# Reordering the openings, the seams and the tail of a feed-forward, convolution, attention and feed-forward kernel

## The chip, the cores and the metric

The kernel runs on one core of one Trainium2 chip. The metric is the device time of one execution in microseconds. All matrix products are done by TensorE (PE); VectorE (DVE), ScalarE (ACT) and GpSimd (POOL) do elementwise work, and SyncE (SP) issues the DMAs. Work on different engines is ordered by semaphores that the program sets and waits for by hand.

## The reference

A block of three layers over 2048 tokens of 1024 features in float32, each added to its input. The first and third are the same feed-forward, the second is a convolution with block attention:

```python
def _L0_ffn_ref(x, weight, bias, gate_w, in_channel_scale, out_channel_scale):
    xf = x.reshape(-1, H)
    router_logits = xf @ gate_w.T
    routing = jax.nn.softmax(router_logits.astype(jnp.float32), axis=1).astype(x.dtype)
    in_scale = routing @ in_channel_scale
    out_scale = routing @ out_channel_scale
    wb = ste_sign(weight)
    out = xf * in_scale @ wb.T * out_scale + bias
    return out.reshape(B, S, -1)

x = x + 0.5 * _L0_ffn_ref(_layernorm(x, axis=-1), ...)
x = x + _L0_attn_ref(_layernorm(x, axis=-1), ...)   # convolution of 3 taps to q, k, v of 256 channels; 16 heads in blocks of 128
x = x + 0.5 * _L0_ffn_ref(_layernorm(x, axis=-1), ...)
```

## The kernel before, in words

**Feed-forward** (`feed_forward`, used twice). The tokens go in 8 blocks of 256 (`NG`), each of two tiles of 128. For a block: the tile is normalised by VectorE (`stats`, GpSimd's `power` for the inverse root, `normalise`), transposed by TensorE in four pieces (`transposes`, one bank of PSUM for blocks from 2 on, so each piece waits until ScalarE's `copy_t` has emptied the one before), multiplied with the gate (`logits`, folded by `logits_back`), turned into a routing by VectorE's `softmax_begin` and `softmax_end`, and transposed back (`routing`). Then, for each of 8 slices of 128 features, TensorE makes the input scale (`in_scale`), VectorE multiplies it in (`scale`), ScalarE rounds it to a high part (`high`) and VectorE takes the low part (`low`). The product with the signed weights has four quarters `q` for a block: two tiles by two halves of 512 outputs. A quarter is `product(g, p, q, 0, 8)`: for each of 8 `k` one matmul with the high and one with the low part, 16 matmuls of 512 columns. Quarters use two banks in turn; a quarter waits until the one two before has been scaled out of its bank by VectorE (`m_scaled`), and `in_scale` waits for a low part made earlier (`lo_done`), since it reuses its bank. GpSimd adds half the bias to the residual (line 299) and the residual to the scaled product (line 309). SyncE stores a block of 1 MB when its four quarters are done.

These steps are software-pipelined by hand: while block g's quarters are multiplied, block g+1 is scaled, g+2 gets its logits and routing, g+3 is normalised and transposed. Each engine's `body(g, p)` writes down its order for one block. The first block is an exception, an opening: block 2's transposes and block 1's routing stand in the middle of quarter 0's product, behind k 5.

**End of the first feed-forward.** Its output is normalised again and goes into `X` for the convolution. The last block goes tile by tile (`last_stats`, `last_normalise`, `difference`), while TensorE already does the part of the convolution that needs only earlier blocks (`early_product`); `first_filter` and GpSimd's `outer_sum` make its filters from a raw load, and `early_data` and `late_data` its data.

**Convolution** (`conv_phase`). It is done in 3 stages of 6 units (`NCH`), unit n having two halves h of 4 chunks, for two results f. Filter i = 4n + 2h + f lies in a ring of 3. In stage 0 the products are single float32 products. In stages 1 and 2 each is made of three products of high and low parts: ScalarE makes the high and VectorE (`finish`, line 1232) the low part of the filter, and VectorE makes the low parts of 16 pieces of data (`second_low`, `third_low`) at each seam. `sums(n)` makes two filters of stage 1 from loaded ones. A load into one of two rooms is issued when `sums` of the pair before last is done. `add(n)` combines the finished unit n into `Y`; for stage 1 these are six operations, of which two work in PSUM and four add into `Y`.

**Attention**, behind it, is not touched.

## Time and profile before

| | us |
|---|---|
| median of 3 runs | 978.25 (975.35 to 980.58) |
| the profiled execution | 976.29 |
| its span, first to last instruction | 974.5 |
| mean granted TensorE clock | 0.986 |

| engine | busy us | share |
|---|---|---|
| TensorE matmul | 907.2 | 93% |
| VectorE | 694.1 | 71% |
| GpSimd | 454.3 | 47% |
| ScalarE | 418.8 | 43% |

The trace is of one execution. Its times count from the first instruction. "Idle before" is the time in which an engine did nothing ahead of an instruction, with the work that released it. The first feed-forward lasts until about 215 us, the convolution until 447, the attention until 805, the second feed-forward to the end.

### The profile page before, as it was taken

Reading aid. Unit: us, or ns where it says so; the run is one execution under the profiler, and the core shown is the slowest. Engines: PE = TensorE matmul, PEld = TensorE weight load, DVE = VectorE, ACT = ScalarE, POOL = GpSimd, SP = SyncE. Lnnn points to the kernel's source line nnn. Section 1 sums busy time; section 2 is a strip of 40 time slices with the busy share of each in tenths; the row PEclk is TensorE's granted clock in tenths of the full one; section 3 lists DMA queues with packets and bytes.
Section 4 is the critical chain, followed back from the end, with each engine's and each line's share of the span. In section 5 each row is a group of like instructions: output and inputs, shape, how many; then the busy total and the mean of one; then the engine's idle time right before and its main releaser. Section 6 shows DMA issues by size and latency. Waiting matters only on the chain.

```text
span 974.5 us, 15517 instructions
## 1 busy us (share of the span) xinstructions
PE 907.2 (93%) x4992; PEld 695.5 (71%) x4992; DVE 694.1 (71%) x1449; ACT 418.8 (43%) x1127; POOL 454.3 (47%) x587
## 2 busy tenths in 40 slices
PE   4799999998999999999989999999999798999997
PEld 3477777775444787887777787887777676877785
DVE  5788887688998888455683686288289786776651
ACT  3534443421234336234773565367256443333331
POOL 1267777787763330000255255247144543555565
PEclk9899999998999999999999999999999998999999
DMA  9433322433234431864012124023244652444333
GB/s 283 182 130 130 130 87 88 144 127 109 98 103 156 162 119 44 313 227 173 1 44 65 44 56 141 1 77 96 94 91 139 212 198 86 145 134 149 130 108 108
DMA packets 43013, 119.98 MB, mean 123 GB/s; under 512 B 7232, under 2 KB 16448, under 8 KB 41536
## 3 DMA queue, kind: packets, MB, share of 16 engines
q1 hardware_dynamic: 42944, 119.11, 37.1%
q8 instruction: 37, 0.61, 0.2%
q14 instruction: 32, 0.26, 0.1%
HBM read 87.64 MB, written 31.46 MB: 122 GB/s over the span
## 4 chain that ended last, share of the span: by engine, by line
PE 70%; DVE 16%; issue 5%; ACT 4%; POOL 4%; DMA 1%; DVEq 0%; POOLq 0%; ACTq 0%
PE a_p_g L1925 19%; PE a_p_g L681 12%; PE f_p_m L681 9%; PE a_p_s L1949 4%; PE c_p_m L1353 3%; PE c_p_m L1355 3%; PE c_p_m L1354 3%; PE c_p_m L1351 3%; PE a_p_o L1973 3%; PE a_p_t L1959 2%; PE f_p_t L622 2%; DVE a_oT_lo L1852 1%; PE a_p_s L622 1%; ACT f_xT L549 1%; ACT a_s L1727 1%
## 5 line engine op out<-in xcount | busy, mean ns | idle before, releaser
L1653 POOL TENSOR_TENSOR a_s<-a_s,a_sums 128x512 f32<-128x512 f32 x64 | 66.6, 1041 | 232.9 <-DVE a_sums L1832 232.9
L309 POOL TENSOR_TENSOR f_y<-f_y,f_res 128x256 f32<-128x256 f32 x128 | 96.9, 778 | 114.8 <-DVE f_y L536 114.0
L1727 ACT ACTIVATE a_s<-a_s,a_nmx 128x128 f32<-128x128 f32 x256 | 99.5, 391 | 48.6 <-DVE a_nmx L1828 48.5
L681 PE MATMUL f_p_m<-f_wsign,f_a_hi 128*128 128x512 f32 x256 | 105.8, 413 | 0.0
L681 PE MATMUL a_p_g<-f_wsign,f_a_hi 128*128 128x512 f32 x256 | 103.2, 403 | 0.0
L681 PE MATMUL f_p_m<-f_wsign,f_a_lo 128*128 128x512 f32 x256 | 101.9, 398 | 0.0
L681 PE MATMUL a_p_g<-f_wsign,f_a_lo 128*128 128x512 f32 x256 | 101.1, 395 | 0.0
L299 POOL TENSOR_TENSOR f_res<-f_res,f_hbias 128x256 f32<-128x256 f32 x128 | 96.0, 771 | 0.0
L1925 PE MATMUL a_p_g<-c_xs_hi,x_room 128*128 128x512 f32 x256 | 94.7, 416 | 0.0
L1353 PE MATMUL c_p_m<-c_vh,c_ring 128*128 128x512 f32 x192 | 75.5, 393 | 5.3 <-issue 3.0
L1351 PE MATMUL c_p_m<-c_vf,c_ring_f 128*128 128x512 f32 (+1 forms) x192 | 73.8, 542 | 1.3 <-DVE c_ring_f L1019 1.1
L1355 PE MATMUL c_p_m<-c_vh,c_ring 128*128 128x512 f32 x192 | 74.8, 389 | 0.0
L1354 PE MATMUL c_p_m<-c_vl,c_ring 128*128 128x512 f32 x192 | 74.8, 389 | 0.0
L1011 POOL TENSOR_TENSOR c_raw<-c_raw 128x256 f32<-128x256 f32 x48 | 46.3, 984 | 53.9 <-DMA c_raw<-in_conv_w_dram 42.1
L1351 PEld LDWEIGHTS c_p_m<-c_vf,c_ring_f 128*128 128x128 f32 x192 | 33.5, 190 | 41.3 <-issue 36.8
L1639 POOL TENSOR_TENSOR a_residual<-a_residual,a_bps 128x256 f32<-128x256 f32 x56 | 41.3, 774 | 42.3 <-DMA a_residual<-x_after_ffn 42.3
L1823 DVE TENSOR_TENSOR a_s<-a_p_s,a_mask 128x512 f32<-128x512 f32 x64 | 43.8, 685 | 20.0 <-PE a_p_s L1949 19.7
L1925 PEld LDWEIGHTS a_p_g<-c_xs_hi,x_room 128*128 128x128 f32 x256 | 48.4, 189 | 13.5 <-issue 0.7
L681 PEld LDWEIGHTS f_p_m<-f_wsign,f_a_hi 128*128 128x128 f32 x256 | 48.9, 191 | 11.9 <-issue 2.1
L681 PEld LDWEIGHTS a_p_g<-f_wsign,f_a_hi 128*128 128x128 f32 x256 | 48.7, 190 | 11.9 <-issue 2.1
L681 PEld LDWEIGHTS a_p_g<-f_wsign,f_a_lo 128*128 128x128 f32 x256 | 48.7, 190 | 8.7
L681 PEld LDWEIGHTS f_p_m<-f_wsign,f_a_lo 128*128 128x128 f32 x256 | 49.0, 192 | 7.9
(223 smaller groups left out, 2204.7 us busy)
## 6 DMA issues: line engine op xcount, KB each, us to landing
c_raw<-in_conv_w_dram SPq DMA_DIRECT2D x24, 768.0 KB, 4.3
f_w_raw<-in_w_t_dram SPq DMA_DIRECT2D x8, 1024.0 KB, 9.3
f_res<-in_x_dram SPq DMA_DIRECT2D x16, 512.0 KB, 3.9
x_after_ffn<-f_y SPq DMA_DIRECT2D x8, 1024.0 KB, 6.1
f_xin<-x_after_attention SPq DMA_DIRECT2D x8, 1024.0 KB, 5.0
f_res<-x_after_attention SPq DMA_DIRECT2D x16, 512.0 KB, 4.1
out_dram<-f_y SPq DMA_DIRECT2D x8, 1024.0 KB, 6.3
f_xin<-in_x_dram SPq DMA_DIRECT2D x7, 1024.0 KB, 5.2
```

The costliest lines, as they stand in the source:

```text
L299: last = pool.tensor_tensor(res[:, t, part], res[:, t, part], hbias[:, part], ALU.add)
L309: last = pool.tensor_tensor(y[:, p, t, part], y[:, p, t, part], res[:, t, part], ALU.add)
L681: last = pe.matmul(p_m[:, q % 2, :], part[p][:, k, q // 2 * P:q // 2 * P + P], wsign[:, k, q % 2 * HALF:q % 2 * HALF + HALF], start=(k == ...
L1011: last = pool.tensor_tensor(self.raw[:, h, 0, part], self.raw[:, h, 0, part], self.raw[:, h, 2, part], ALU.add)
L1351: last = pe.matmul(out[:, quads], conv.half(i)[:, cols], vf[:, f, k, quads], start=start, stop=stop)
L1353: pe.matmul(out, ring[:, slot, 0, cols], vh[:, f, k, :], start=start, stop=False)
L1354: pe.matmul(out, ring[:, slot, 0, cols], vl[:, f, k, :], start=False, stop=False)
L1355: last = pe.matmul(out, ring[:, slot, 1, cols], vh[:, f, k, :], start=False, stop=stop)
L1653: pool.tensor_tensor(s[:, r], s[:, r], sums[:, r].unsqueeze(2).broadcast_to([P, 4, P]), ALU.mult).then_inc(probs_ready, 1)
L1727: done = act.activation(s[:, r, h, :], s[:, r, h, :], ACT.Exp, bias=nmx[:, r, h:h + 1], scale=SCALE, accum_out=sums[:, r, h:h + 1])
L1823: dve.tensor_tensor(s[:, r], p_s[:, u % 2, :].rearrange("p (h t) -> p h t", h=4), mask[:].unsqueeze(1).broadcast_to([P, 4, P]), ALU.add).t ...
L1925: mm = pe.matmul(p_g[:, bank, :], a, b, start=n == 0, stop=n == len(pairs) - 1)
```

## The change

In words, in the order of the diff:

- The last quarter's residual of each feed-forward is added by VectorE (`last_sum`), not by GpSimd. In the first, GpSimd's second filter sum moves behind its bias sum.
- The last block of the second feed-forward is stored in three pieces (`store_last`): tile 0, and the two halves of tile 1. The first keeps its store.
- The opening of both (`opening`): quarter 1's product no longer stands behind block 2's transposes. Its k 0 to 3 are taken in turns with quarter 0's k 4 to 7 ahead of the first transpose, and its other k stand between the transposes, the input scales and the logits. `copy_t(2, ...)` moves into ScalarE's body with its copies and high parts between, and `copy_logits(2)` moves from q = 0 to q = 1. Two k of quarter 2 come ahead of its input scale.
- In the first feed-forward, `normalise(2, 0)` stands ahead of `softmax_end(1)`.
- In the convolution, `add` of stage 1 is split into `combine` (two operations) and `accumulate` (four), and the low part `finish(n, 1)` stands between. At both seams low parts of filters come ahead of part of the low parts of the data.

The core of the diff:

```diff
+        def store_last():
+            g, p = NG - 1, (NG - 1) % 2
+            sp.wait_ge(y_done, 4 * g + 2)
+            sp.dma_start(dstv[g][:, 0, :], y[:, p, 0, :]).then_inc(y_stored[p], 16)
+            for q, h in enumerate((slice(0, HALF), slice(HALF, D))):
+                sp.wait_ge(y_done, 4 * g + 3 + q)
+                sp.dma_start(dstv[g][:, 1, h], y[:, p, 1, h]).then_inc(y_stored[p], 16)
...
-                pool.wait_ge(res_biased, 4 * g + q + 1)
-                pool.wait_ge(m_scaled, 4 * g + q + 1)
-                for part in halves(h):
-                    last = pool.tensor_tensor(y[:, p, t, part], y[:, p, t, part], res[:, t, part], ALU.add)
-                last.then_inc(y_done, 1)
+                if q < 3 or not late(g):
+                    pool.wait_ge(res_biased, 4 * g + q + 1)
+                    pool.wait_ge(m_scaled, 4 * g + q + 1)
+                    for part in halves(h):
+                        last = pool.tensor_tensor(y[:, p, t, part], y[:, p, t, part], res[:, t, part], ALU.add)
+                    last.then_inc(y_done, 1)
+                if q == 3 and X is not None and late(g):
+                    conv.outer_sum(pool, 1)
...
-                if q == 2 and X is not None and late(g):
-                    conv.outer_sum(pool, 1)
...
+        def last_sum():
+            g, p = NG - 1, (NG - 1) % 2
+            dve.wait_ge(res_biased, 4 * NG)
+            dve.wait_ge(m_scaled, 4 * NG)
+            dve.wait_ge(y_done, 4 * NG - 1)
+            dve.tensor_tensor(y[:, p, FT - 1, HALF:D], y[:, p, FT - 1, HALF:D], res[:, FT - 1, HALF:D], ALU.add).then_inc(y_done, 1)
...
                 if first_round(g) and q == 0:
+                    copy_t(2, 0, 0)
+                    copy_t(2, 0, 1)
                     copy_routing(1, 1)
+                    copy_t(2, 0, 2)
+                    high(1, 1, 0)
+                    copy_t(2, 0, 3)
+                    high(1, 1, 1)
+                    continue
...
-                if q == 0 and exists(g + 2):
+                if q == (1 if first_round(g) else 0) and exists(g + 2):
                     copy_logits(g + 2)
...
+        def opening(g, p):
+            out_scale(g, p, 0)
+            product(g, p, 0, 0, 4)
+            for k in range(4, KD):
+                product(g, p, 1, k - 4, k - 3)
+                product(g, p, 0, k, k + 1)
+            transposes(2, 0, 0)
+            product(g, p, 1, 4, 5)
+            transposes(2, 0, 1)
+            product(g, p, 1, 5, 6)
+            routing(1)
+            transposes(2, 0, 2)
+            in_scale(1, 1, 0)
+            transposes(2, 0, 3)
+            product(g, p, 1, 6, 7)
+            in_scale(1, 1, 1)
+            out_scale(g, p, 1)
+            logits(2, 0)
+            product(g, p, 1, 7, KD)
+            in_scale(1, 1, 2)
+            logits_back(2)
+            in_scale(1, 1, 3)
+            transposes(3, 1, 0)
...
-            for q in range(4):
+            if first_round(g):
+                opening(g, p)
+            for q in range(2 if first_round(g) else 0, 4):
                 out_scale(g, p, q)
...
+                ahead = 2 if first_round(g) and q == 2 else 0
+                product(g, p, q, 0, ahead)
...
             f.stats(2, 0)
+            f.normalise(2, 0)
             f.softmax_end(1)
-            f.normalise(2, 0)
             f.stats(3, 1)
             group_loop(dve, f.body)
             f.last_normalise(0)
             conv.early_data(dve, Xp, 1)
+            f.last_sum()
             f.last_stats(1)
...
             sums(2 * NCH)
-            for r in range(8):
+            for r in range(6):
                 second_low(r)
             finish(2 * NCH, 0)
+            for r in range(6, 8):
+                second_low(r)
+            finish(2 * NCH, 1)
             sums(2 * NCH + 1)
             for r in range(8, 12):
                 second_low(r)
-            finish(2 * NCH, 1)
-            second_low(12)
             finish(2 * NCH + 1, 0)
-            for r in range(13, 16):
+            for r in range(12, 16):
                 second_low(r)
+            finish(2 * NCH + 1, 1)
             add(NCH - 1)
-            finish(2 * NCH + 1, 1)
             sums(2 * NCH + 2)
             for n in range(2 * NCH + 2, 4 * NCH):
                 if n + 1 < 4 * NCH:
                     sums(n + 1)
                 finish(n, 0)
                 if n % 2:
-                    add((n - 3) // 2)
+                    combine((n - 3) // 2)
                 finish(n, 1)
-            for r in range(8):
+                if n % 2:
+                    accumulate((n - 3) // 2)
+            for r in range(6):
                 third_low(r)
             for n in range(4 * NCH, PAIRS):
                 finish(n, 0)
                 if n == 4 * NCH:
-                    for r in range(8, 12):
+                    for r in range(6, 12):
                         third_low(r)
-                if n % 2:
+                if n == 4 * NCH + 1:
+                    combine((n - 3) // 2)
+                elif n % 2:
                     add((n - 3) // 2)
                 finish(n, 1)
+                if n == 4 * NCH + 1:
+                    accumulate((n - 3) // 2)
```

## Rows read from the trace of the kernel before

**Rows 1.** The page, part 1: busy us (share of the span), instructions.

```profile
PE 907.2 (93%) x4992; PEld 695.5 (71%) x4992; DVE 694.1 (71%) x1449; ACT 418.8 (43%) x1127; POOL 454.3 (47%) x587
```

**Rows 2.** Waits of TensorE: us in total, times, longest us.

```profile
PE f_p_t L622 <- DVE f_xin L365: 13.9, 2, 11.0
...
PE f_p_n L700 <- DVE f_res L471: 3.0, 1, 3.0
```

**Rows 3.** Timeline of TensorE, first opening: start us, us, instruction, idle before.

```profile
36.96 1.12 PE L622 MATMUL f_p_t<-ident,f_xin 128*128 128x128 f32 x4 [2.93 <-DVE f_xin L365]
...
54.43 0.36 PE L662 MATMUL c_p_m<-f_rT,f_ics 128*128 128x256 f32 x1 [0.74 <-DVE f_a_lo L423]
```

**Rows 4.** Timeline of VectorE, same stretch.

```profile
35.14 1.76 DVE L365 TENSOR_SCALAR f_xin<-f_xin,f_mv,f_rstd 128x1024 f32<-128x1024 f32 x2
36.94 2.47 DVE L344 BATCH_NORM_STATS2 f_st<-f_xin 128x6 f32<-128x512 f32 x4
...
46.30 0.42 DVE L423 TENSOR_TENSOR f_a_lo<-c_p_m,f_a_hi 128x256 fp32r<-128x256 f32 x1 [1.28 <-ACT f_a_hi L566]
...
53.87 0.41 DVE L423 TENSOR_TENSOR f_a_lo<-c_p_m,f_a_hi 128x256 fp32r<-128x256 f32 x1
```

**Rows 5.** Timeline of GpSimd, same stretch.

```profile
34.02 0.69 POOL L279 TENSOR_TENSOR f_rstd<-f_vpe,f_minus_half 128x2 f32<-128x2 f32 x1 [19.18 <-DVE f_vpe L356]
```

**Rows 6.** Stretches: start:end, us, TensorE busy (matmuls), granted clock, DMA, GB/s.

```profile
29.95:33.36 3.41, 3.41 (x10) 0.51 0.77 309
33.36:36.78 3.42, 0.67 (x3) 0.99 0.01 6
...
40.19:43.60 3.41, 1.88 (x12) 0.99 0.00 0
...
811.60:815.01 3.41, 1.42 (x13) 1.00 0.22 26
```

**Rows 7.** Timeline of ScalarE, second opening.

```profile
810.39 0.58 ACT L549 COPY f_xT<-a_p_s 128x512 f32<-128x512 f32 x1 [0.81 <-PE a_p_s L622]
```

**Rows 8.** The chain that ended last, second opening: start us, us, work.

```profile
819.05 3.21 PE a_p_g L681 x8
...
822.39 1.82 PE a_p_g L681 x8
```

**Rows 9.** Timeline of VectorE, second opening.

```profile
817.45 0.42 DVE L423 TENSOR_TENSOR f_a_lo<-a_p_o,f_a_hi 128x256 fp32r<-128x256 f32 x1 [2.02 <-ACT f_a_hi L566]
```

**Rows 10.** Timeline of all engines, end of the first feed-forward.

```profile
217.63 2.83 POOL L299 TENSOR_TENSOR f_res<-f_res,f_hbias 128x256 f32<-128x256 f32 x2
...
221.98 1.28 DVE L459 BATCH_NORM_STATS2 f_nst<-f_y 128x6 f32<-128x512 f32 x2 [2.09 <-POOL f_y L309]
```

**Rows 11.** One line's instructions: ns min/median/max, first and last start, shapes.

```profile
L1206 DVE SCALAR_TENSOR_TENSOR X<-X,c_room x8: 681/1212/1219, 240.5 to 292.3; 128x512 f32<-128x512 f32 x8
```

**Rows 12.** Timeline of TensorE, stage 0 of the convolution.

```profile
274.14 14.34 PE L1351 MATMUL c_p_m<-c_vf,c_ring_f 128*128 128x512 f32 x32 [0.37 <-DVE c_ring_f L1019]
```

**Rows 13.** The chain that ended last, first seam of the convolution.

```profile
320.81 4.26 DMA c_raw<-in_conv_w_dram
```

**Rows 14.** Timeline of TensorE, units 7 and 12 of the convolution.

```profile
332.74 0.50 PE L1353 MATMUL c_p_m<-c_vh,c_ring 128*128 128x512 f32 x1 [1.16 <-DVE c_ring L1232]
...
380.11 0.47 PE L1353 MATMUL c_p_m<-c_vh,c_ring 128*128 128x512 f32 x1 [0.79 <-issue]
...
390.28 0.50 PE L1353 MATMUL c_p_m<-c_vh,c_ring 128*128 128x512 f32 x1 [1.17 <-DVE c_ring L1232]
```

**Rows 15.** Timeline of all engines, the end.

```profile
968.61 1.40 POOL L309 TENSOR_TENSOR f_y<-f_y,f_res 128x256 f32<-128x256 f32 x2 [1.03 <-DVE f_y L536]
970.03 0.40 SPq L226 DMA_DIRECT2D out_dram<-f_y  x1
```

**Rows 16.** DMA issues: number, KB each, median us to landing.

```profile
x_after_attention<-a_residual SPq DMA_DIRECT2D x56, 128.0 KB, 2.3
```

**Rows 17.** Stretches of the end: us, engines' busy us, granted clock, DMA share, GB/s.

```profile
973.00:973.50 0.50, 0.00 (x0) 0.00 (x0) 0.00 (x0) 0.00 (x0) 0.00 (x0) 0.50 1.00 401
```

More of the change, by code:

```diff
@@ L244, in stored @@
         def stored():
-            for count in y_stored:
-                sp.wait_ge(count, 16 * (NG // 2) + 1)
-        return SyncSteps(load_x, load_tiles, load_gate, load_scales, load_w, load_bias, load_res, store, stored, body)
+            for p, count in enumerate(y_stored):
+                pieces = 2 if X is None and p == (NG - 1) % 2 else 0
+                sp.wait_ge(count, 16 * (NG // 2 + pieces) + 1)
+        return SyncSteps(load_x, load_tiles, load_gate, load_scales, load_w, load_bias, load_res, store, store_last, stored, body)
     def pool(pool):
@@ L539, in vector @@
         return VectorSteps(start, constants, tile_stats, mean_var, stats, normalise_tile, normalise, scale_parts,
-                           softmax_begin, softmax_end, softmax, scale, low, None if X is None else last_stats, None if X is None else last_normalise,
+                           softmax_begin, softmax_end, softmax, scale, low, last_sum, None if X is None else last_stats, None if X is None else last_normalise,
                            None if X is None else difference, body)
@@ L701, in normed @@
             last.then_inc(n_full, 1)
+        def opening(g, p):
[21 more added lines that the diff above has]
+            transposes(3, 1, 0)
         def body(g, p):
-            for q in range(4):
+            if first_round(g):
+                opening(g, p)
+            for q in range(2 if first_round(g) else 0, 4):
                 out_scale(g, p, q)
-                first = first_round(g) and q == 0
-                if first:
-                    product(g, p, q, 0, KD - 2)
-                    for piece in range(4):
-                        transposes(2, 0, piece)
-                        if piece < 2:
-                            product(g, p, q, KD - 2 + piece, KD - 1 + piece)
-                    routing(1)
+                ahead = 2 if first_round(g) and q == 2 else 0
+                product(g, p, q, 0, ahead)
                 if exists(g + 1):
@@ L728, in body @@
                 else:
-                    if not first:
-                        product(g, p, q, 0, 4)
+                    product(g, p, q, ahead, 4)
                     if exists(g + 1):
@@ L736, in body @@
                         logits_back(g + 2)
-                    if not first:
-                        product(g, p, q, 4, KD)
+                    product(g, p, q, 4, KD)
                 if q and exists(g + 3):
@@ L857, in _ @@
                 f.sign_w(k)
-            for q in range(4):
-                f.copy_t(2, 0, q)
             group_loop(act, f.body)
@@ L1776, in _ @@
             s2.exponent(1)
-            for piece in range(4):
-                s2.copy_t(2, 0, piece)
             group_loop(act, s2.body)
```

33 lines of the change are left out of this document (19 added, 14 removed).

## The prediction

> **What bounds the kernel now.** The page comes first. TensorE is busy for 907.2 of 974.5 us, VectorE for 71% (the page; [rows 1]). So an edit can only win where TensorE stands still or runs at the low clock. The list of who waited for whom gives where: 2.9 us for a normalised tile in the first opening, 3.0 us for the last tile's normalised residual, and a handful of waits of about 1 us on the convolution's filters [rows 2, 14]. Second, the timelines of TensorE and VectorE at each of these places tell what came last, and third, the stretches with a low granted clock tell what the standstill costs afterwards. Elsewhere the products run back to back at 0.227 us each (8 in 1.82 us [rows 8]), and none falls away. The five places are separate, and behind each TensorE hardly waits, so I add their shifts.
>
> **1. Opening of the first feed-forward (-4.0 us).** Before, quarter 0's product is cut by the transposes of block 2; after, 12 matmuls of quarter 1 are put ahead of the first transpose, and quarter 1's other k go between transposes, scales and logits. TensorE before: it stops at 33.97, waits 2.93 us for the normalised tile, and gets the fifth input scale of block 1 (the one that waits for a low part) at 54.43 [rows 3]. What ends last on that way is VectorE: low part 0 at 46.30, from there a queue without a wait over 0.5 us to low part 3 at 53.87, whose end releases 54.43 [rows 4]. This queue keeps its order, so TensorE at 54.43 moves by as much as the 46.30 moves.
>
> When does it start now? The variance is ready at 33.87, GpSimd's power ends at 34.71 [rows 5]. `normalise(2, 0)` now stands ahead of `softmax_end`, so it runs from 34.8 to 36.5 (1.76 us [rows 4]) instead of 36.9. The eight small operations of `softmax_end` took 1.4 us from 33.78 and 2.1 us from 50.55, when GpSimd was at work; it halves the bias in the new place, so they end at 37.9 to 38.6. Statistics of block 3 take 3.0 us [rows 4]: 40.9 to 41.6. TensorE in the meantime: 24 matmuls from 29.47. The clock is low from 29.95 to 33.36 [rows 6], in which 8 go at 0.43 us; the other 14 take 3.2 us, so the first transpose stands at 36.55, just as the tile is ready. The extra matmuls cost nothing there: they lie in the 2.93 us hole. Then the transposes are paced by ScalarE's copy, 1.39 us apart as in the second opening (0.58 and 0.81 idle [rows 7]): 36.6, 38.0, 39.4 and, after the copy of the routing, 40.6; input scale 0 is out at 39.9, before VectorE is free for it. So VectorE scales at 41.2 (middle), and low part 0 follows 0.86 us later (as 49.35 to 50.21) at 42.1, against 46.30: 4.2 us. In the before it took 1.71 us there, because ScalarE stood behind the logits; `copy_logits(2)` now comes one quarter later. I take off 0.2 us for block 3's normalising beside GpSimd's bias sum: 4.0, between 3.2 and 4.6.
>
> What is late next: TensorE has quarter 2's k 0 to 3 to do, from the release of the bank (VectorE's sum of quarter 0, 48.75 before, 44.7 now) to 47.1, and then stands until 50.4 for low part 3. That is the standstill of before, put in one piece of about 3 us.
>
> **2. Opening of the second (-2.7 us).** No wait for a tile there: the first transpose came at 808.36 and now comes at 805.63 + 24 x 0.227 = 811.1, so 2.7 us later. Before, four transposes 1.4 us apart, the copies of scales and routing and the slow logits brought low part 0 to 817.45 and low part 3 to 825.38, and TensorE, delayed by quarter 1 at the low clock, reached the scale only at 826.66, 0.86 us after it could [rows 7 to 9]. Now: transposes at 811.1 and 812.5, routing at 813.3, its copy until 814.05, scale 0 on TensorE at 814.2, VectorE at 814.5, low part 0 at 815.4: 2.0 us earlier, low part 3 ends at 823.8, TensorE goes on at 823.9 instead of 826.66, if nothing else is late. 2.7, between 1.8 and 3.2.
>
> **3. The granted clock (+1.7 us).** Stretches in which TensorE was busy for 0.67 and 1.42 us of 3.4 us were followed by one or two of that length at 0.51 of full speed; one with 1.88 us was not [rows 6]. Each low stretch of 3.4 us loses 1.7 us of products (8 take 3.21 instead of 1.82 us [rows 8]). Both new standstills (3.3 and 3.1 us) can fall either side of that; I count one drop of 3.4 us in the two openings, and none or two for the range (0 to +3.4). The low stretch at 815 to 822 belongs to the before and is already inside term 2.
>
> **4. End of the first feed-forward (-0.9 us).** Before, the chain is: VectorE's product of the last quarter, GpSimd's filter sum (215.81, 1.85 us), bias sum (2.83 us), residual sum (1.40 us) until 221.94, statistics, power, normalising until 225.18, TensorE at 225.24 [rows 2, 10]. Now GpSimd's bias sum goes ahead of the filter sum, and VectorE adds the residual itself behind `early_data(1)`, which ends at 219.88. The sum of 128x512 takes 0.68 us, or 1.21 where GpSimd works beside it [rows 11]; so the statistics start at 220.5 to 221.1 against 221.98. Queued behind the new wait on VectorE are the statistics, two differences, two filters and the data; its semaphore has been given by about 217.7 if the bias sum takes the 1.85 us that the filter sum took in that place. The filter sum moves to 217.7 to 220.5, and its first reader is at 225.10: hidden. I take 0.9, range 0 to 1.4.
> The Trainium skill speaks against this part (SBUF — State Buffer, Who interferes with whom): a VectorE operation with two SBUF inputs and a GpSimd operation that reads SBUF block each other for the whole instruction. The trace agrees with the two lengths of 0.68 and 1.21 us, and with 5.33 us for the filter sums at 228.87; by the rule alone the gain would be 0.3 less than by the middle of the rows.
> Behind it the first stage of the convolution is VectorE's: its period is 14.70 us without a wait, TensorE waits 0.37 us in each [rows 12]. So TensorE gains what VectorE gains there, though its own low clock at 224.5 to 231.3 may go: that is no gain.
>
> **5. The convolution's seams (-1.0 us).** From stage 0 to 1, the filters' low parts put ahead of data let unit 6 start at 309.8 instead of 310.67, and its second half without the 1.25 us wait: 2.1 us. But from 302.93 to 320.7 VectorE has no wait over 0.1 us, and the order of its work is all that changes: `sums(14)` still ends at 320.8. This releases a filter load (4.26 us), GpSimd's sum, and `sums(16)` at 326.61, and behind it the filter half that TensorE needs at 328.60 [rows 13]. So the 2.1 us are waited for there. The split of `add` gives the next half 2.4 us earlier and takes away the wait of 1.16 us at 332.74 [rows 14], but VectorE is again full until 335.3, where unit 8's filter is due at 335.5: 0.1 us is left. Together 0.1.
> From stage 1 to 2: before, `finish(23,1)` at 373.91 stands behind the sums; ScalarE has its high part at 371.84, so VectorE loses 0.35 us. Unit 12's first low part then comes two data parts earlier, at 378.5 instead of 379.33: TensorE starts unit 12 0.85 us earlier (0.79 us wait [rows 14]). Its second filter comes after all 12 data parts as before, 0.35 us later, which takes that back. Then `combine` and the low part of filter 25 go ahead of the four sums: ready at 388.2, TensorE needs it at 389.2, instead of 390.28 with 1.17 us wait. Behind that stage 2 is TensorE's. So 1.1 there, less what the first seam may cost: 1.0, between 0.2 and 2.5.
>
> **6. The end (-2.4 us).** Before: product until 968.46 on VectorE, GpSimd 968.61 to 970.01, store of 1 MB issued 970.03, data moving until 973.53 at about 400 GB/s, end at 974.5 [rows 15, 17]. Now VectorE adds in 0.69 us and ends at 969.2 (-0.8). The last store holds 256 KB: 2.6 us of data become 0.65 (-1.95) if the half rows of 2 KB go as fast. The bound on the other side is the 2.3 us median of 128 KB stores against 4.0 here [rows 15, 16], a slope of 2.0 us per MB, so -1.5. The other 768 KB are issued at 962.4 and 966.2 and done before. Sum 2.3 to 2.75; I take 2.4, range 1.9 to 2.9.
> The Trainium skill (DMA: Bandwidth & Descriptors, Bandwidth) has a rule against pieces: batch DMAs to 1 MiB or more. It would count if the queue were full; the trace shows none of it in use from 967 to 970. No term changes.
>
> **Sum.** -4.0 - 2.7 + 1.7 - 0.9 - 1.0 - 2.4 = -9.3 us. The profiled execution took 976.29 us (span 974.5, 1.8 around it): 967.0. It lies 1.96 us below the median of 978.25 (975.35 to 980.58), from which it would be 968.95. Where the clock falls differs between executions, so I take the middle: 968.0. About 0.5% (4.9 us) is what a measurement of this kernel can tell from no change.
>
> **The rivals.**
> A, the forecast: gains of 7.5 to 11.5 us, 0.50.
> B, the openings stay at full clock, or the first conv seam keeps its 2.1 us since the load at 320.81 comes earlier than I count: -11.0 to -14, about 965.5. For it: TensorE is busy in the new seams with products, not only transposes. Against: the holes of 3 us. 0.14.
> C, ScalarE or the clock takes part of the openings back: the copy of the fourth transposed piece now stands behind `high(1, 1, 0)`, which waits for VectorE's scale. The logits, their copy and their fold are ready at about 45.4, VectorE wants them at 45.6 in the first opening; each microsecond more there is one lost. With two low stretches besides: 9.3 - 1.7 - 2 = 5.6, so 972. 0.20.
> D, the change doesn't do what it says: the holes are only moved. If low part 0 of both openings comes no earlier, since transposes that stand behind 24 matmuls are 2.7 us later, terms 1 and 2 are 0 to -1 and the clock costs 0 to +1.7: -3.5 to -4.5, 974.2. For it: VectorE bounds both. Against: four waits on the way to low part 0 are removed in the first. 0.13.
> E, slower than before: the standstill in one piece lets the clock fall in the rounds behind both openings and it stays low there. Against: in each of its places before, it came back after at most two stretches [rows 6]. Each microsecond at low clock costs half of one, so it decides from the point at which more than 22 us of low clock are added; over both first rounds (some 20 us each) the price is 20 + the 1.7 not counted twice: -11 + 20, so 986. 0.03.
> Range: 962.0 to 974.0 leaves out E, half of D and the end of B. Faster by more than 0.5%: A, B and most of C, 0.85; within: 0.12; slower: 0.03.
>
> **What would show it.** Term 1: first transpose of block 2 at about 36.6 behind 24 matmuls, VectorE's low part 0 near 42, TensorE idle up to 3.3 us before a scale, and quarter 3's start 4 us earlier. Term 2: the same at 10 us behind the opening's start. Term 3: a stretch at 0.5 of the clock right behind the idle one. Term 4: statistics right behind VectorE's own sum, POOL's filter sum beside the data. Term 5: no wait at unit 6, but 1.5 us at unit 7's start and 0.4 in it. Term 6: three stores, the last 2.3 us from issue to landing. The prediction is wrong if VectorE's queue in the openings is not the order-giver, or if the load behind `sums(14)` comes earlier.

## The result, and the profile after

| | before | after |
|---|---|---|
| median of four runs each, same chip | 977.53 us | 966.09 us (963.99 to 969.31) |
| profiled execution | 976.29 | 963.99 |
| its span | 974.5 | 962.2 |

The ratio is 0.9884, 95% interval 0.9843 to 0.9924: 11.3 us less, between 7.4 and 15.3. In a second series (six runs of after, eleven of before) it was 0.9892 (0.9869 to 0.9916). The forecast of 968.0 stands inside both intervals, near the end of the smaller gain.

In what follows, "before" and "after" are the kernels without and with the change, and "the hole" is the wait of TensorE for low part 3 of block 1 in each new opening.

The page of after. Columns: busy us (share of the span) and instructions; [rows 1] has those of before. TensorE is busy for 8 us less in a span 12.3 us shorter.

```profile
PE 899.2 (93%) x4992; PEld 690.5 (72%) x4992; DVE 695.2 (72%) x1451; ACT 418.3 (43%) x1127; POOL 451.6 (47%) x583
```

The list of TensorE's waits in after (us in total, times, longest). Against [rows 2], the 2.93 us for a tile in the first opening and the 3.0 us for the last tile are no longer in it, and two waits of 2.4 us for a low part (line 433) are new, one in each opening.

```profile
...
PE c_p_m L686 <- DVE f_a_lo L433: 2.7, 2, 2.4
PE c_p_m L1409 <- DVE c_ring L1273: 2.5, 3, 1.3
...
PE a_p_o L686 <- DVE f_a_lo L433: 2.4, 1, 2.4
```

**First opening.** TensorE's timeline in after: the last product ahead of the fifth input scale, that scale, two of the products behind it, quarter 3's output scale. It answers to [rows 3], where the scale stood at 54.43.

```profile
45.82 0.39 PE L705 MATMUL f_p_m<-f_wsign,f_a_lo 128*128 128x512 f32 x1
48.57 0.55 PE L686 MATMUL c_p_m<-f_rT,f_ics 128*128 128x256 f32 x1 [2.36 <-DVE f_a_lo L433]
48.92 0.63 PE L705 MATMUL f_p_m<-f_wsign,f_a_hi 128*128 128x512 f32 x1
49.35 0.63 PE L705 MATMUL f_p_m<-f_wsign,f_a_lo 128*128 128x512 f32 x1
...
52.36 0.48 PE L693 MATMUL c_p_m<-f_ocs,f_rT 128*128 128x512 f32 x1
```

And VectorE's, with low part 0 (46.30 before, [rows 4]), the six rows of `softmax_end` (lines 405 to 417) and low part 3, which releases the scale:

```profile
39.86 0.42 DVE L433 TENSOR_TENSOR f_a_lo<-c_p_m,f_a_hi 128x256 fp32r<-128x256 f32 x1 [0.44 <-ACT f_a_hi L583]
...
44.36 0.42 DVE L433 TENSOR_TENSOR f_a_lo<-c_p_m,f_a_hi 128x256 fp32r<-128x256 f32 x1 [0.15 <-ACT f_a_hi L583]
44.70 0.16 DVE L405 TENSOR_REDUCE f_r_sum<-f_r_exp 128x2 f32<-128x16 f32 x1
44.89 0.17 DVE L407 RECIPROCAL f_r_max<-f_r_sum 128x2 f32<-128x2 f32 x1
45.09 0.17 DVE L409 TENSOR_TENSOR f_r_exp<-f_r_exp,f_r_max 128x16 f32<-128x16 f32 x1
45.30 0.60 DVE L412 CAST f_r_hi<-f_r_exp 128x16 fp32r<-128x16 f32 x1
45.94 0.73 DVE L415 COPY f_rt<-f_r_hi 128x16 f32<-128x16 f32 x2
46.58 0.24 DVE L417 TENSOR_TENSOR f_rt<-f_r_exp,f_r_hi 128x16 f32<-128x16 f32 x2
...
48.01 0.41 DVE L433 TENSOR_TENSOR f_a_lo<-c_p_m,f_a_hi 128x256 fp32r<-128x256 f32 x1
```

The scale moved by 5.86 us, of which 1.57 us is the start-up, ahead of anything the change touches (VectorE's subtraction in `softmax_begin` at 30.80 before, 29.23 after): 4.29 us between the two kernels, at clocks that were not equal (see term 1 below). Behind the hole the products start 0.43 us apart, not 0.23. The stretches (start:end, us, TensorE busy, granted clock, DMA, GB/s) give the clock:

```profile
44.00:48.00 4.00, 2.13 (x9) 1.00 0.01 5
48.00:52.00 4.00, 3.43 (x9) 0.57 0.39 125
52.00:56.00 4.00, 4.00 (x25) 1.00 0.02 8
```

TensorE stood still, then it was granted half the clock (1.2 GHz) for 3.4 us, then 2.4 GHz again.

**Second opening.** The scale stands at 815.42 behind a like hole, and the clock falls at 816.2. The first row is that of before, where it stood at 826.66; [rows 8] shows the slow products ahead of it.

```profile
826.66 0.28 PE L662 MATMUL a_p_o<-f_rT,f_ics 128*128 128x256 f32 x1
...
815.42 0.36 PE L686 MATMUL a_p_o<-f_rT,f_ics 128*128 128x256 f32 x1 [2.35 <-DVE f_a_lo L433]
```

**End of the first feed-forward.** VectorE's own sum (line 468), the statistics right behind, GpSimd's bias and filter sums (lines 308, 1052), and TensorE's transposes, which stood at 225.24 before. [rows 2, 10] has the chain of before, except for its GpSimd residual sum, which is the first row here:

```profile
220.54 1.40 POOL L309 TENSOR_TENSOR f_y<-f_y,f_res 128x256 f32<-128x256 f32 x2
...
211.33 1.86 POOL L308 TENSOR_TENSOR f_res<-f_res,f_hbias 128x256 f32<-128x256 f32 x2
213.15 2.84 POOL L1052 TENSOR_TENSOR c_raw<-c_raw 128x256 f32<-128x256 f32 x2
...
215.33 1.21 DVE L468 TENSOR_TENSOR f_y<-f_y,f_res 128x512 f32<-128x512 f32 x1
216.57 1.28 DVE L476 BATCH_NORM_STATS2 f_nst<-f_y 128x6 f32<-128x512 f32 x2
...
219.83 0.66 PE L724 MATMUL f_p_n<-ident,f_res 128*128 128x128 f32 x4 [2.11 <-DVE f_res L488]
```

**First conv seam.** GpSimd's filter sum behind the load that `sums(14)` releases, `sums(16)`, and TensorE's waits at unit 7, in it, and at unit 8. The last two rows are unit 12 of after, in the second seam (380.11 before, [rows 14]), and unit 8 of before.

```profile
319.61 1.43 POOL L1052 TENSOR_TENSOR c_raw<-c_raw 128x256 f32<-128x256 f32 x2 [6.20 <-DMA c_raw<-in_conv_w_dram]
...
321.07 0.70 DVE L1262 TENSOR_TENSOR c_p_u<-c_raw 128x512 f32<-128x512 f32 x1 [3.56 <-POOL c_raw L1052]
...
317.07 0.47 PE L1409 MATMUL c_p_m<-c_vh,c_ring 128*128 128x512 f32 x1 [1.26 <-DVE c_ring L1273]
323.02 0.50 PE L1409 MATMUL c_p_m<-c_vh,c_ring 128*128 128x512 f32 x1 [0.25 <-DVE c_ring L1273]
329.78 0.47 PE L1409 MATMUL c_p_m<-c_vh,c_ring 128*128 128x512 f32 x1 [1.02 <-DVE c_ring L1273]
...
377.74 0.47 PE L1409 MATMUL c_p_m<-c_vh,c_ring 128*128 128x512 f32 x1 [1.23 <-issue]
...
335.64 0.39 PE L1353 MATMUL c_p_m<-c_vh,c_ring 128*128 128x512 f32 x1
```

**The end.** VectorE's last product, its sum, the issue of the last store, and the data of it (columns as above, all engines idle, clock, DMA share, GB/s). [rows 15 to 17] have these of before.

```profile
958.21 0.69 DVE L553 TENSOR_TENSOR f_y<-a_p_g,f_oscale 128x512 f32<-128x512 f32 x1 [3.16 <-PE a_p_g L705]
959.00 0.69 DVE L468 TENSOR_TENSOR f_y<-f_y,f_res 128x512 f32<-128x512 f32 x1
959.71 0.33 SPq L234 DMA_DIRECT2D out_dram<-f_y  x1
...
960.50:961.00 0.50, 0.00 (x0) 0.00 (x0) 0.00 (x0) 0.00 (x0) 0.00 (x0) 1.00 0.89 348
```

**Where 12.3 us of span went**, by differences between the starts of the same instructions in both traces:

| stretch | before | after | gain |
|---|---|---|---|
| to the first product of the first feed-forward (not in the change) | 29.47 | 28.07 | 1.40 |
| opening 1: from there to VectorE's scaling of quarter 3 | 32.44 | 29.38 | 3.06 |
| rest of its quarters | 153.08 | 153.07 | 0.01 |
| end of it, to the first sum into `Y` | 29.61 | 28.67 | 0.94 |
| from there to `combine` of stage 1's fifth unit | 125.72 | 125.39 | 0.33 |
| from there to the last sum into `Y` | 78.03 | 76.94 | 1.09 |
| attention (not in the change) | 356.97 | 354.93 | 2.04 |
| opening 2: from its first output scale to quarter 3's scaling | 28.77 | 28.05 | 0.72 |
| rest of its quarters | 133.68 | 133.71 | -0.03 |
| last product on VectorE to the end | 6.73 | 3.99 | 2.74 |

8.9 us lie in stretches that the change touches, together with what the clock did there; 3.4 us lie in the two stretches that it doesn't touch.

### The profile page after: what moved, and what is told of

Read it like the earlier page. It is cut to its first block, busy times and chain, and to the rows that moved or that the text cites. A ratio compares the mean times of both kernels' runs of the same rounds, so it can differ in the third digit from the quotient of the medians.

```text
span 962.2 us, 15524 instructions
## 1 busy us (share of the span) xinstructions
PE 899.2 (93%) x4992; PEld 690.5 (72%) x4992; DVE 695.2 (72%) x1451; ACT 418.3 (43%) x1127; POOL 451.6 (47%) x583
## 4 chain that ended last, share of the span: by engine, by line
PE 74%; DVE 13%; issue 5%; ACT 4%; POOL 2%; DMA 1%; DVEq 0%; ACTq 0%; POOLq 0%
PE a_p_g L1980 19%; PE a_p_g L705 12%; PE f_p_m L705 10%; PE c_p_m L1407 4%; PE c_p_m L1409 4%; PE c_p_m L1411 4%; PE c_p_m L1410 4%; PE a_p_s L2004 3%; PE a_p_o L2028 3%; PE a_p_t L2014 2%; DVE a_oT_lo L1906 1%; PE f_p_t L646 1%; PE a_p_s L646 1%; ACT f_xT L566 1%; ACT a_s L1783 1%
## 5 line engine op out<-in xcount | busy, mean ns | idle before, releaser
L319 POOL TENSOR_TENSOR f_y<-f_y,f_res 128x256 f32<-128x256 f32 x124 | 94.0, 779 | 109.5 <-DVE f_y L553 108.8
```

The costliest lines, as they stand in the source:

```text
L319: last = pool.tensor_tensor(y[:, p, t, part], y[:, p, t, part], res[:, t, part], ALU.add)
```

## The experiments

Eleven kernels ran, before and after among them. Where the order of work and the clock are the same, the stretches of the table agree between executions within 0.1 us, and the first seam within 0.2, so one profile each decides much that a median of runs, which scatters by 2 to 5 us, doesn't. The table gives for each profile five stretches of the table above, with the number of low-clock stretches (each 3.4 us at half the clock, so up to 1.7 us lost; one at the very start of opening 1 is counted too) in brackets, and for the first seam the time from the end of stage 0's last product on TensorE to `combine` of unit 6.

| profile | opening 1 | end of FF 1 | first seam | second seam, stage 2 | opening 2 | end | median us |
|---|---|---|---|---|---|---|---|
| before | 32.44 (2) | 29.61 | 18.70 | 78.03 | 28.77 (2) | 6.73 | see text |
| openings only | 30.61 (3) | 29.64 | 18.86 | 78.03 | 26.47 (0) | 6.74 | 972.75 |
| conv only | 34.15 (3) | 29.61 | 18.31 | 76.93 | 27.02 (0) | 6.75 | 976.68 |
| ends only | 34.23 (4) | 28.68 | 18.88 | 78.02 | 28.78 (2) | 4.02 | 974.97 |
| after | 29.38 (2) | 28.67 | 18.39 | 76.94 | 28.05 (1) | 3.99 | 966.09 |
| after, again | 29.75 (2) | 28.68 | 18.21 | 76.92 | 28.04 (1) | 3.94 | 966.54 |
| filler | 28.18 (1) | 28.69 | 19.84 | 76.90 | 26.44 (0) | 3.98 | 966.60 |
| filler, again | 28.15 (1) | 28.68 | 19.32 | 76.96 | 26.48 (0) | 3.99 | 964.38 |
| softmax later | 27.08 (0) | 28.68 | 18.33 | 76.91 | 25.37 (0) | 3.98 | 963.46 |
| sums(14) first | 29.74 (2) | 28.68 | 17.19 | 76.95 | 28.05 (1) | 4.02 | 964.67 |
| three undone | 29.89 (1) | 28.13 | 18.29 | 76.92 | 28.02 (1) | 5.94 | (970.22) |
| three mended | 27.04 (1) | 28.14 | 17.15 | 76.90 | 25.34 (0) | 4.00 | 960.67 |
| routing behind | 26.82 (1) | 28.14 | 17.10 | 76.90 | 25.37 (0) | 3.96 | 959.23 |

The kernel before had a median of 978.68 beside the first three and the first filler, 975.75 beside "after, again" to "sums(14) first", 977.57 beside the last three. "Three undone" was run once, so its 970.22 is no median.

**1. The openings alone.** The kernel before with the diff's changes to `opening`, TensorE's and ScalarE's `body`, the copies, and this on VectorE:

```diff
-            f.softmax_end(1)
             f.normalise(2, 0)
+            f.softmax_end(1)
```

> The kernel before with the two openings alone: quarter 1 in the seam, block 2's normalising ahead of softmax_end, the copies and logits in their new order. The convolution, both ends and the stores are as before. My account: in the first opening the fifth input scale is released at about 48.6 instead of 54.4 (5.8 us, of which some 1.5 us is where the start-up fell), in the second 2.4 us are won against the start of that phase, and each opening has a hole of about 2.4 us ahead of that scale, behind which 3.4 us run at the low clock (1.4 to 1.7 us lost in each). Together -3.6 us when both drops come, -6.7 when none does; in the median of several executions about 973. The rival, that the holes were only moved: low part 0 of block 1 in the first opening no more than 1 us earlier than 46.3, and a time within 1.5 us of the kernel before.

972.75 us, ratio 0.9944 (0.9929 to 0.9958): 5.5 us less. The scale stood at 48.95 behind 2.35 us, and at 821.15 in the second, behind 2.35 us, but there the clock stayed high. That the holes were only moved is refuted: low part 0 stood at 10.64 us behind VectorE's subtraction, in before at 15.50. And a hole alone doesn't decide about the clock.

**2. The convolution alone.** The diff's part in `conv_phase`.

> The kernel before with the reordered convolution seams alone. My account: -0.1 to -0.5 us in the seam from stage 0 to 1 (the start of unit 8, counted from the end of stage 0) and -1.1 us in the seam from 1 to 2, together -1.2 to -1.6 us, so about 976. TensorE doesn't wait at unit 6, but 1.2 to 1.5 us at unit 7. The rival, that the first seam keeps its 2.1 us: unit 8 starts 2 us earlier, about 974.5, and there is no wait of over 0.5 us at unit 7.

976.68 us, ratio 0.9972 (0.9953 to 0.9991), too coarse to tell the two apart. The stretches do: -1.1 in the second seam (76.93), and in the first 18.31, where profiles in the old order have 18.70, 18.86 and 18.88: about -0.5, with 0.2 us of scatter. TensorE waited 1.28, 0.24 and 1.07 us at unit 7, in it and at unit 8. The rival of 2.1 us falls.
This trace also corrects my second term. Its second opening is in the old order, and it is the only one of the kernels with that order where the clock stayed high. TensorE's timeline there:

```profile
824.56 0.35 PE L662 MATMUL a_p_o<-f_rT,f_ics 128*128 128x256 f32 x1 [0.76 <-DVE f_a_lo L423]
```

The opening's first output scale stood at 805.05, so the scale came 19.51 us behind it. In before that was 21.34 (826.66 - 805.32), in the changed orders with the hole 18.96 to 18.99. At an equal clock the reordering wins 0.54 us there, not 2.4.

**3. The two ends alone.** `last_sum`, the order of GpSimd's sums, and the store in pieces.

> The kernel before with the two ends alone: VectorE adds the residual of the last quarter, GpSimd's second filter sum stands behind its bias sum, the last block is stored in three pieces. My account: -0.9 us at the last tile of the first feed-forward (VectorE's sum takes 0.7 us alone and 1.2 us beside GpSimd) and -2.4 to -2.8 us from VectorE's last product to the end, so about 974.5. The rival, that VectorE's sum and GpSimd stand in each other's way: the last tile's transposes no earlier than before, and 0.9 us less gain.

974.97 us, ratio 0.9964 (0.9950 to 0.9979): 3.5 us less; 0.93 in the end of the first feed-forward and 2.71 in the end. As expected; the two effects were told apart only in experiment 7.

**4. Products in the hole.** After, with nine matmuls of 512 columns into `p_n`, which nothing reads then, ahead of the scale that waits:

```diff
                     product(g, p, q, ahead, 4)
+                    if ahead:
+                        filler(g, p, q, 9)
```

> The changed kernel with nine products more in each opening, just ahead of the input scale for which TensorE waits 2.4 us. They go to a bank that nothing reads, so no result changes; 9 x 0.227 = 2.04 us, less than the hole. If the low clock behind the hole is the answer to TensorE's standstill, the stretch behind it stays at full clock: products at 0.227 instead of 0.43 us, quarter 3 starts 1.4 us earlier in the first opening and 1.7 us in the second, and the kernel comes out some 3 us below the changed one (about 963). The scale itself comes no earlier. The rival, that the clock falls there for another reason (the transposes and 128-column work ahead, or all that was done in the opening): the stretch is low just the same, and the time stays at 966 or is up to 0.5 us longer.

> The kernel with nine products more in each opening once more, since its first profile showed both openings at full clock and yet no shorter time (966.6), with low stretches at 497 to 505 and 764 to 768 instead. If filling the hole is worth what it saves in the openings, the median is 1.5 to 3 us below the changed kernel's of this same call; if the drops come back elsewhere, within 0.7 us of it. Both openings are at full clock from the extra products on, either way.

TensorE's timeline of the first run: the nine products, the scale, and the next transposes, which stand behind the half quarter.

```profile
47.98 2.21 PE L729 MATMUL f_p_n<-f_wsign,f_a_hi 128*128 128x512 f32 x9
50.52 0.36 PE L686 MATMUL c_p_m<-f_rT,f_ics 128*128 128x256 f32 x1 [0.32 <-DVE f_a_lo L433]
...
52.55 0.60 PE L646 MATMUL f_p_t<-ident,f_xin 128*128 128x128 f32 x4
```

From the scale to those transposes 2.03 us, in after 3.44. In both profiles both openings stayed at 2.4 GHz behind the filler, 1.2 to 1.6 us shorter in the first and 1.6 in the second, with the scale no earlier. The openings without a hole in experiments 5, 8 and 9 had no drop there either, six of six. So the standstill is what the clock answers to here, and the two drops cost about 3 us. The medians don't confirm that: 966.60 (ratio 0.9876, interval 0.9849 to 0.9903) beside 966.09 in another series, and 964.38 (0.9885, 0.9860 to 0.9910) beside 966.54 in the same one. Part of it is seen: both filler profiles are 0.9 to 1.6 us longer in the first conv seam, where the load for its first filters came later (VectorE waited 3.56 and 3.10 us for it, 2.03 in after). Why it came later is open.

**5. softmax_end later.** After, and in the first block's turn VectorE does (in words, not the kernel's lines):

```diff
 scale 2, softmax_begin, low 2
-softmax_end, scale 3, y of quarter 1, scale 4, low 3, low 4, scale 5
+scale 3, low 3, y of quarter 1, scale 4, low 4, scale 5, softmax_end
```

> The changed kernel, and in the first block's turn VectorE does softmax_end of block 2 behind the fifth scale, not between the third and the fourth, and low part 3 ahead of quarter 1's product. The eight small operations take 2.0 us in the first opening (1.4 in the second) on VectorE's way to low part 3, for which TensorE waits 2.4 us. If that order is what makes the hole, the scale is released 1.5 to 2 us earlier, the hole is 0.3 to 0.9 us, and quarter 3 begins 1 to 1.9 us earlier in the first opening and 1 to 1.4 in the second, less at most 0.5 us for the routing of block 2, which now is ready only about when TensorE wants it; the two openings -2 to -3.3 us and the drop of the clock behind the hole gone, in all 962 to 964. The rival: quarter 3 gets late for the routing by as much, so that both openings are as long as before at the same clock (966).

963.46 us, ratio 0.9853 (0.9828 to 0.9879); beside it after had 966.54. TensorE's timeline (fifth scale, quarter 3's output scale, routing):

```profile
48.15 0.36 PE L690 MATMUL c_p_m<-f_rT,f_ics 128*128 128x256 f32 x1
...
50.54 0.48 PE L697 MATMUL c_p_m<-f_ocs,f_rT 128*128 128x512 f32 x1
...
52.08 0.44 PE L677 MATMUL c_p_m<-ident,f_rt 128*128 128x128 f32 x2 [0.95 <-DVE f_rt L417]
```

There is no wait at the scale, no fall of the clock behind it, and 0.95 us for the routing instead, twice what I allowed. Against the filler kernels (same clock) the openings are 1.1 us shorter each, against after 2.3 to 2.7. So the hole was VectorE's order of work. The edit moved more than `softmax_end`: low part 3 now also stands ahead of quarter 1's product and a scale. It came 1.20 us behind low part 2, where it came 3.65 behind it in after (44.36 to 48.01). Of these 2.45 us `softmax_end` took at most 2.05 (44.70 to 46.75); the two weren't run apart.

**6. sums(14) first.** After, with `sums(14)` ahead of `add(5)`, and the first filter of unit 7 finished ahead of `sums(15)`:

```diff
             finish(2 * NCH + 1, 1)
-            add(NCH - 1)
             sums(2 * NCH + 2)
+            add(NCH - 1)
+            finish(2 * NCH + 2, 0)
```

> The changed kernel, and in the first seam of the convolution sums(14) stands ahead of add(5) and the first filter of unit 7 ahead of sums(15), the high part of it ahead of ScalarE's scalings. My account of the first seam (sums(14), the load that it releases, GpSimd's sum, sums(16) end last) says: the load is issued 1.2 us earlier (at 2.8 us before what it is now against the end of stage 0 plus 10.4), TensorE's wait of 1.26 us at unit 7 goes, the waits of 0.25 and 1.02 us behind it stay below 0.6 together, and unit 8 starts 1.2 us earlier; 965. If VectorE being full is the bound by itself and not the load, the first wait goes and comes back at the start of unit 8, which comes at the same time: 966.

964.67 us, ratio 0.9876 (0.9854 to 0.9898). TensorE's remaining waits in the seam, and `sums(16)`:

```profile
322.68 0.50 PE L1413 MATMUL c_p_m<-c_vh,c_ring 128*128 128x512 f32 x1 [0.18 <-DVE c_ring L1275]
329.50 0.47 PE L1413 MATMUL c_p_m<-c_vh,c_ring 128*128 128x512 f32 x1 [1.06 <-DVE c_ring L1275]
...
320.73 0.70 DVE L1264 TENSOR_TENSOR c_p_u<-c_raw 128x512 f32<-128x512 f32 x1 [1.78 <-POOL c_raw L1052]
```

Stage 0 ended at 305.35 here and at 304.49 in after. So `sums(16)` came 1.20 us earlier (15.38 against 16.58) and unit 8 1.14 (24.15 against 25.29). The wait at unit 7 is gone. The 1.06 us at unit 8 stayed, against my 0.6 for both, but the chain moved as a whole, as the theory of the load says.

**7. Three parts undone.** After, with `softmax_end(1)` ahead of `normalise(2, 0)` again, GpSimd's own residual sum in the first feed-forward (the filter sum behind it), and the last store in one piece.

> The changed kernel with three parts of it undone, each in a stage of its own. (1) softmax_end of block 1 stands ahead of block 2's normalising again, in the first opening. VectorE waits 0.87 us for the root at present; the eight small operations fill that, the tile is ready some 0.5 us later and VectorE's statistics end 0.8 us earlier. If low part 0 hangs on VectorE's queue and on the routing's copy alike, the first opening is as long as now within 0.3 us at the same clock (29.4 to 29.8 from the first product to quarter 3's scaling with one low stretch); if the earlier tile is what brought the gain, it is 0.5 to 1.4 us longer. (2) In the first feed-forward GpSimd adds the last quarter's residual itself again, but the filter sum stays behind it. Its bias sum ends at 213.2 in the changed kernel's trace, the residual sum would end at about 214.7, before VectorE's early_data ends (215.3), so the statistics start at 215.4 instead of 216.57 and the end of the first feed-forward takes 27.5 us instead of 28.68. That says that the whole of term 4 came from the filter sum's move. The rival, that VectorE's taking over is what gives the gain: 29.2 to 29.6 us. (3) The last block is stored in one piece of 1 MB again, VectorE's sum stays. By my step the pieces are worth 1.9 us of the 2.74: from VectorE's last product to the end 5.9 us instead of 3.99; the rival, that the pieces bring only the slope of the small stores, 1.5 us: 5.5.

Opening 1 took 29.89 us. Its one low stretch is behind the hole and none is at the start, so a better measure is VectorE's own: low part 0 came 10.66 us behind the subtraction, in after 10.63, and the scale 19.41, in after 19.34. That move alone is worth nothing. The end: 5.94 against 3.99, so the pieces bring 1.95 and VectorE's sum 0.79. The end of the first feed-forward is 28.13, neither of my two values. GpSimd's residual sum there and the statistics behind it:

```profile
215.81 2.72 POOL L314 TENSOR_TENSOR f_y<-f_y,f_res 128x256 f32<-128x256 f32 x2
...
218.57 1.29 DVE L471 BATCH_NORM_STATS2 f_nst<-f_y 128x6 f32<-128x512 f32 x2 [0.62 <-POOL f_y L314]
```

The sum takes 2.72 us beside VectorE's `early_data`, not 1.40 as in before (220.54), so the statistics wait 0.62. Still it is 0.54 better than VectorE's own sum. Of the 1.48 us from 29.61 to 28.13 all comes from the filter sum's new place, and VectorE's taking over gives 0.54 of it back.

**8. Three mended.** After with the edits of 5 and 6, and GpSimd's residual sum of 7.

> The changed kernel with three edits: softmax_end of block 2 later in both openings (as in the third kernel of the last series), sums(14) earlier in the first conv seam (as in the fourth), and in the first feed-forward the last residual by GpSimd, with the filter sum behind it. If they add up: openings 27.1 and 25.4 us as there, first seam 1.1 us shorter than the changed kernel's, end of the first feed-forward 27.5 instead of 28.68; 3.1 + 1.1 + 1.1 = 5.3 us under the changed kernel's 966, so about 961. If GpSimd's sum is not what I take it for, about 962.3.

960.67 us, ratio 0.9829 (0.9808 to 0.9850). The edits add up, each stretch as it was alone; the end of the first feed-forward is 28.14 as in experiment 7, not the 27.5 that was hoped for.

**9. The routing behind four k.** The kernel of experiment 8, and TensorE's `routing(2)` stands behind the first half of quarter 3, its copy behind a high part.

> The kernel with the three edits, and in both openings the routing of block 2 stands behind the first four k of quarter 3 on TensorE, its copy behind the seventh high part on ScalarE. TensorE waited 0.95 us for it in either opening, while quarter 3's operands were ready. If that wait is all that is left, both openings are 0.9 to 1.0 us shorter: 26.1 and 24.4, and the time 1.9 us below the kernel with three edits, about 959. The rival, that VectorE is the bound there and the wait comes back at the scales of quarter 3 or of the next block: the openings shorter, but the rest of the feed-forward longer than 153.0 and 133.7 us by what is gained, and no change in the time.

959.23 us, ratio 0.9810 (0.9790 to 0.9830), the best of all, though its interval overlaps that of 8. The 0.95 us wait is gone, a wait of 0.2 to 0.3 us for a low part is new. The openings missed the forecast: 26.82 and 25.37 us, not 26.1 and 24.4, so to quarter 3's scaling the wait came back as the rival said. But opening and rest together are 0.6 us shorter in the first feed-forward and 0.4 in the second: 1.0, not 1.9. The gain shows mainly in the next blocks (152.48 for 152.89, 133.12 for 133.55), where the rival had a loss.

**The changed kernel again.**

> The changed kernel once more, for a second profile of it and a median beside the next three. 966 to 968. By the table of stages (the same stage agrees within 0.1 us between executions where the clock is the same) the end of the first feed-forward, the seams, the stages and the end should show the same lengths as in its first profile; only stretches at the low clock, 1.7 us each, may fall elsewhere. If the openings always cost two drops, as in the first profile, they show here too; the other view is that they fall by chance.

966.54 us. Both openings had their drop again, behind the same scale. In the attention, which no kernel alters, zero to three low stretches fell, for 354.9 to 359.5 us: the 2.04 us of the first table go with one such stretch in before and none in after.

## Why the prediction was right, and where it wasn't

The sum was -9.3 us, and the stretches that the change touches gave -8.9. That they lie so near is partly luck: the order alone gave less than terms 1 and 2 say, low clock in before's own openings made up for it, the new drops cost more than term 3, and terms 5 and 6 gave more.

**Term 1, first opening.** Predicted 4.0 to the scale, measured 4.29. The first transpose stood at 34.96 behind 24 matmuls and without a wait, which is my 36.6 less the start-up. Low part 0 gained 4.9 us (46.30 - 39.86 - 1.57) where I had 4.2, and VectorE's queue lost 0.6 of it again on the way to low part 3. The 4.29 us aren't the order's alone. Before had a low stretch on the way (36.8 to 40.2), which "ends only", in the same old order, hadn't there; its first input scale (first row) came 12.45 us behind the subtraction (29.96), that of before (second row) 13.37:

```profile
42.41 0.58 PE L679 MATMUL c_p_m<-f_rT,f_ics 128*128 128x256 f32 x1 [1.22 <-ACT f_rT L578]
44.17 0.39 PE L662 MATMUL c_p_m<-f_rT,f_ics 128*128 128x256 f32 x1 [1.22 <-ACT f_rT L561]
...
36.80:40.20 3.40, 3.24 (x12) 0.50 0.02 5
```

So about 0.9 us are the clock's by an estimate from these rows, and some 3.4 the order's. No profile of the old first opening is without a low stretch: its fifth scale came 23.6, 25.4 and 25.9 us behind the subtraction in three profiles, in the new order with the hole 19.3 to 19.4 in all. The hole, one piece as foretold, was 2.36 us and not 3. That "VectorE is the order-giver" was right, and it was also where the next gain lay: `softmax_end` stands in that queue ahead of low part 3 (experiment 5).

**Term 2, second opening.** Predicted 2.7, measured 2.37 in this pair, and the step behind it failed. I took the 21.34 us of before as the old order's length, while 1.8 of them were the low clock: 6.8 us at half (815.1 to 821.9) lose 3.4 us of products and made TensorE late for its own scale; I had even noted the 0.86 us. "Low part 0 2.0 us earlier" was 1.2 at equal clock, and VectorE's queue from there to the scale grew from 8.12 to 8.77 us. The order is worth 0.54 us. The rest is a clock that fell in two of the three profiles of the old order.

**Term 3, the clock.** +1.7 predicted, for one drop; there were two, and from the scale to quarter 3's scaling they cost 1.4 and 1.6 us against the filler's openings. That they belong to the hole was right (experiment 4), and that they may fail to come too (experiment 1). The median gained more than the pair's 8.9 us. Before has drops of its own, of which this profile had few: opening 1 is 32.4 to 34.2 us long in three profiles of the old order, 29.4 to 29.9 in four of after's.

**Term 4, end of the first feed-forward.** Predicted 0.9, measured 0.94, and the step was wrong: the gain was put down to both edits, but one of them costs. That the size fits is luck. The sum at VectorE took 1.21 us, the upper of my two bounds, and its being there costs 0.54; the order of GpSimd's sums alone gives 1.48. The Trainium skill's rule (SBUF — State Buffer, Who interferes with whom), that a VectorE operation with two SBUF inputs and a GpSimd operation reading SBUF hold each other up, is borne out on both sides: 0.69 becomes 1.21 us for VectorE's sum, 1.40 becomes 2.72 for GpSimd's. I used it against the VectorE sum alone.

**Term 5, the seams.** Second seam 1.1 as predicted. First 0.5 by VectorE's `combine`, and by TensorE's unit 8 it was 0.6 (335.64 - 309.72 against 329.78 - 304.49), not 0.1. The step that failed is that `sums(14)` "still ends" where it did. VectorE's low parts of the data run beside GpSimd's filter sums, in before eight in a row (first row), in after six (second row), and two later in 1.81 us; eight took 4.90 us at 374.51 in before, where GpSimd was idle:

```profile
302.93 7.03 DVE L1239 TENSOR_TENSOR c_vl<-X,c_vh 128x512 fp32r<-128x512 f32 x8
...
297.81 4.76 DVE L1280 TENSOR_TENSOR c_vl<-X,c_vh 128x512 fp32r<-128x512 f32 x6
```

From the first of them to `sums(14)` it is 16.57 us in before (319.50) and 16.03 in after (313.84). Against the end of stage 0 `sums(14)` came 0.43 us earlier and `sums(16)` 0.31; where the rest came from wasn't traced. TensorE's waits were where I had them, but for 1.02 us at unit 8: none at unit 6, 1.26 us at unit 7 (1.5) and 0.25 in it (0.4). That `sums(14)` and its load end last was the right reason, shown by moving them.

**Term 6, the end.** 2.4 predicted, 2.74 measured: pieces 1.95 (my upper value, since 256 KB moved at 348 GB/s and landed 2.0 us after its issue, not 2.3) and sum 0.79. The bound from the slope of small stores was too low.

**Rivals.** B had about 965.5, nearer to the measured 966.09 than my 968.0. It needed both openings at full clock or 2 us in the first seam: neither in this pair. C's mechanism, ScalarE's order, isn't seen in either opening; its clock part is. D is refuted by low part 0, 4.9 us earlier in the first opening, and by experiment 1. E: behind the holes the clock came back after 3.4 us, once after 6.8.

## What to carry to other kernels

When two executions of one kernel are compared, cut them at the starts of the same instructions and count the low-clock stretches in each piece before an edit gets the credit: here 0.54 us of reordering looked like 2.4. Where a wait is moved rather than removed, look at what its engine does just ahead of what is waited for; here eight small operations whose result nobody needed yet made most of the hole. A bundle of edits in one place should be undone one at a time, since one of them may take back a third of what another gives.

## What the runs showed of the hardware

A single standstill of 2.4 us was followed by 3.4 us at 1.2 GHz (once 6.8) in nine of ten openings that had one, and by none in the tenth; the same opening with the standstill filled by unused products kept 2.4 GHz in four of four. Small operations of VectorE are slowed by GpSimd much as large ones are: the copy of 16 columns (line 415, two of them) took 0.73 us while GpSimd added (45.12 to 46.56 in after), the cast 0.60, against 0.25 and 0.17 where GpSimd was idle (at 20.64 and 20.43 us).
